# Attention with heads of eight numbers: scores from two f32r parts, stored twice in half of the rows of TensorE's array, in place of three bf16 parts in all of them

## The reference

```python
def causal(x):                       # H=16, Hd=8, L=1024, B=2
    q, k, v = split(layernorm(x) @ W_attn + b_attn)
    scores = einsum('bhqd,bhkd->bhqk', q, k) / sqrt(8)
    scores = where(tril, scores, -inf)
    return einsum('bhqk,bhkd->bhqd', softmax(scores), v) @ W_proj + b_proj

def encoder(x):
    q, k, v = x @ Wq.T + bq, x @ Wk.T + bk, x @ Wv.T + bv     # reshape to 32 heads of [1024, 8]
    att = softmax(einsum('nqd,nkd->nqk', q, k)) + batch_pos
    att_out = einsum('nqk,nkd->nqd', att, v) @ Wo.T + bo
    ...
```

## Time and profile before

| | us |
|---|---|
| runs | 2842.07, 2851.0, 2852.22 (median 2851.0) |
| profiled execution, own time | 2846.07 |
| its span | 2844.2 |
| `a1`: first product of `a1x` to the end of its units | 288.7 to 575 |
| `b1`: SP enters `b1x`, first product, end of its units | 1613.9, 1632.7, 2055 |
| TensorE busy, share of the span | 86% |
| mean granted clock of TensorE | 0.906 |

### The profile page before, as it was taken

The page is one execution under the profiler, slowest core; times in us unless marked ns, Lnnn a source line. Parts: engine busy times, 40 slices in busy tenths (PEclk is TensorE's granted clock), DMA queues, the critical chain, the costliest instruction groups (busy, mean ns, idle before and its releaser), DMA issues. The chain is left out here.

```text
span 2844.2 us, 41392 instructions
## 1 busy us (share of the span) xinstructions
PE 2441.5 (86%) x12171; PEld 1441.7 (51%) x12236; DVE 2095.6 (74%) x4112; ACT 1423.1 (50%) x3001; POOL 623.5 (22%) x605
## 2 busy tenths in 40 slices
PE   5994889949978999779996499899858899969998
PEld 3772344327756555357773322222125555437776
DVE  3994777538968999279995188788337899738998
ACT  2552356615521777146664036666611377616665
POOL 2324000013317000124445100000003400013443
PEclk7996799969979999889997769999978999979999
DMA  1212222112212000034432611211032000004443
GB/s 64 81 55 72 55 61 56 25 36 107 76 37 49 1 1 1 8 128 141 151 144 48 156 43 28 53 29 29 15 39 78 8 1 1 9 7 157 146 151 117
DMA packets 110486, 175.34 MB, mean 62 GB/s; under 512 B 58738, under 2 KB 81138, under 8 KB 98466
## 3 DMA queue, kind: packets, MB, share of 16 engines
q1 hardware_dynamic: 93428, 171.23, 20.7%
q10 hardware_dynamic: 16896, 2.10, 0.5%
HBM read 145.43 MB, written 12.78 MB: 56 GB/s over the span
## 5 line engine op out<-in xcount | busy, mean ns | idle before, releaser
L1496 DVE TENSOR_REDUCE b1x_maxima<-b1x_m_bank 128x1 f32<-128x512 f32 x512 | 317.9, 684 | 82.7 <-PE b1x_m_bank L1414 82.7
L1536 ACT ACTIVATE b1x_probs<-b1x_e_bank 128x1024 f32<-128x1024 f32 x256 | 248.2, 1021 | 119.4 <-PE b1x_e_bank L1432 112.4
L1496 DVE TENSOR_REDUCE a1x_maxima<-a1x_m_bank 128x1 f32<-128x512 f32 (+3 forms) x384 | 190.3, 551 | 72.6 <-PE a1x_m_bank L1417 48.6
L1414 PE MATMUL b1x_m_bank<-b1a_k_slot,b1a_q_slot 96*128 96x512 bf16 x512 | 190.4, 412 | 23.3 <-DMA b1x_v_slot<-b1a_v_aug 20.4
L1536 ACT ACTIVATE a1x_probs<-a1x_e_bank 128x1024 f32<-128x1024 f32 (+1 forms) x192 | 147.3, 809 | 101.4 <-PE a1x_e_bank L1435 79.0
L1432 PE MATMUL b1x_e_bank<-b1a_q_slot,b1a_k_slot 128*128 128x512 bf16 x475 | 145.7, 385 | 8.4 <-issue 4.1
L1414 PE MATMUL a1x_m_bank<-a1a_k_slot,a1a_q_slot 96*128 96x512 bf16 (+3 forms) x384 | 120.2, 351 | 21.2 <-DMA a1x_v_slot<-a1a_v_aug 19.5
L1448 PE MATMUL b1x_o_bank<-b1x_probs,b1x_v_slot 128*32 128x512 f32 x1024 | 137.7, 610 | 0.7 <-ACT b1x_probs L1536 0.7
L1414 PEld LDWEIGHTS b1x_m_bank<-b1a_k_slot,b1a_q_slot 96*128 96x128 bf16 x512 | 41.5, 98 | 181.8 <-DVE b1x_maxima L1496 129.8
L585 ACT ACTIVATE g1e_high<-g1e_hidden 128x512 fp32r<-128x512 f32 x128 | 80.9, 632 | 90.4 <-DVE g1e_hidden L618 90.2
L585 ACT ACTIVATE g2e_high<-g2e_hidden 128x512 fp32r<-128x512 f32 x128 | 81.0, 633 | 90.1 <-DVE g2e_hidden L618 90.0
(11 more groups left out here) (556 smaller groups left out, 6503.7 us busy)
## 6 DMA issues: line engine op xcount, KB each, us to landing
g1e_share<-scratch_combine SPq DMA_DIRECT2D x32, 1024.0 KB, 4.8
g2e_share<-scratch_combine SPq DMA_DIRECT2D x32, 1024.0 KB, 4.8
f1e_share<-scratch_combine SPq DMA_DIRECT2D x9, 1024.0 KB, 4.9
f2e_share<-scratch_combine SPq DMA_DIRECT2D x9, 1024.0 KB, 4.9
b1e_window<-scratch_bias_table SPq DMA_DIRECT2D x16, 320.0 KB, 4.6
a1a_k_slot<-scratch_k_parts SPq DMA_DIRECT2D x24, 192.0 KB
a1a_q_slot<-scratch_q_parts SPq DMA_DIRECT2D x72, 64.0 KB
b1a_k_slot<-scratch_k_parts SPq DMA_DIRECT2D x24, 192.0 KB
```

The costliest lines, as they stand in the source:

```text
L1414: mm = pe.matmul(bank[:, 0:width], q_slot[s][0:MAX_ROW, qt // 4, hh, chunk(qt % 4, 128)], k_slot[s][0:MAX_ROW, hh, k0:k0 + width], start=T ...
L1496: dve.tensor_reduce(maxima[:, k0 // NC, col:col + 1], bank[:, 0:width], AX, ALU.max).then_inc(m_taken, 1)
L1536: act.activation(probs[g % 2][:, 2 * pair:2 * pair + 2, 0:width], e_bank[pair][:, :, 0:width], ACT.Exp, scale=scale).then_inc(exp_done, 1)
```

## The change

- PARTS is 2 and the parts are f32r (ACT makes the high part with the bias added, one DVE operation the low one). Three products of parts by 8 numbers are 24 rows; they are stored **twice** (COPIES = 2), so a head takes 48 rows (MAX_ROW), and the exponential's `scale` is divided by COPIES. The two rows of the maximum follow. Even heads lie in rows 0 to 49, odd ones in rows 64 to 113.
- A score product (lines 1373 and 1391) covers one half of the array's rows; the tiles are ordered by head, so that neighbours lie in different halves. The mask products (1376, 1394) are as before: bf16, over all 128 rows.
- The parts stay on chip. `Narrow.load` copies them from `q_parts` and `k_parts` into the slots: 32 DMAs per group in the causal block, 48 in the encoder (24 for q and 24 for k, of 8x16x64 numbers; a piece that lies together has 64 numbers, 256 bytes). The encoder's weights are permuted on the host so that eight rows of one number index lie together. `v_slot` and its loads go; the value products read `v_aug`.
- Groups 0 and 1 are loaded earlier: group 0 by SP in `qkv_in_parts` (causal) or in the turn of the values (encoder), group 1 by SP in `narrow_values` (causal) or by ACT's queue in `relative_bias` (encoder). Group 2 is loaded at the start of `narrow_attention`, around `rows(0)`.
- No loop: the 16 halves are written out. At every second half SP waits for the end of the half before, loads group + 2, and only then does `rows(half + AHEAD)` (AHEAD is 2 in the causal block and 1 in the encoder) and `store(half)`.
- The first pass is shared out by a planner (`due`: a tile is worth its width + 32, a turn 256): 63 items ahead of the first unit in the causal block, 50 in the encoder, and then about 4.1 per unit in the encoder, none in the last units. Both turns stand six tiles behind the last tile of their half.
- POOL cuts the maximum with two operations in place of five, four DMAs write it.

```diff
-PARTS = 3
+PARTS = 2
+COPIES = 2
+MAX_ROW = 24 * COPIES
...
+    ROW_PARTS = {"q": (0, 1, 0), "k": (0, 0, 1)}
+    def load(self, queue, group, operand):
+        parts, slot = ((self.q_parts, self.q_slot) if operand == "q" else (self.k_parts, self.k_slot))
+        s = group % SLOTS
+        for e in range(4):
+            b, n = (4 * group + e) // NH, (4 * group + e) % NH
+            at = 64 * (e % 2)
+            if self.positions_split:
+                for i in range(3 * COPIES):
+                    part = self.ROW_PARTS[operand][i % 3]
+                    queue.dma_start(slot[s][at + HD * i:at + HD * i + HD, e // 2, :].bitcast(F32),
+                                    parts[:, part, b * L + 64 * n:b * L + 64 * n + 64].bitcast(F32)
+                                    ).then_inc(self.slot_loaded[s], 16)
+                continue
...
-    scale = HD ** -0.5 if causal else 1.0
+    scale = (HD ** -0.5 if causal else 1.0) / COPIES
...
+            narrow.load(sp, 2, "q")
+            rows(0)
+            narrow.load(sp, 2, "k")
+            for half in range(1, AHEAD):
+                rows(half)
+            for half in range(HALVES):
+                group = half // 2 + SLOTS - 1
+                if SLOTS <= group < GROUPS and half % 2 == 0:
+                    sp.wait_ge(pv_done, last_unit[half - 1] + 1)
+                    narrow.load(sp, group, "q")
+                    narrow.load(sp, group, "k")
+                if half + AHEAD < HALVES:
+                    rows(half + AHEAD)
+                store(half)
...
+                rows = slice(64 * (hh % 2), 64 * (hh % 2) + MAX_ROW)
                 diagonal = causal and k0 + width == (qt + 1) * 128
+                mm = pe.matmul(bank[:, 0:width], q_slot[s][rows, hh // 2, chunk(qt, 128)],
+                               k_slot[s][rows, hh // 2, k0:k0 + width], start=True, stop=not diagonal)
                 if diagonal:
                     mm = pe.matmul(bank[:, width - 128:width], ident_bf[:], mask[:, 0, :],
                                    start=False, stop=True)
...
+                for a in ((0, 1) if pair == 0 else (1, 0)):
+                    rows = slice(64 * a, 64 * a + MAX_ROW + PARTS)
                     diagonal = causal and lo == kt * 128
+                    mm = pe.matmul(e_bank[pair][:, a, 0:width], k_slot[s][rows, pair, chunk(kt, 128)],
+                                   q_slot[s][rows, pair, lo:lo + width], start=True, stop=not diagonal)
                     if diagonal:
                         mm = pe.matmul(e_bank[pair][:, a, 0:128], ident_bf[:], mask[:, 1, :],
                                        start=False, stop=True)
```

More of the change, by code:

```diff
@@ L1118, in prepare_values @@
         self.memset(pool, self.v_heads[:, :, :, :, HD], 1.0)
[L1120 to L1128, removed]
 def qkv_in_parts(nc, tag, dram, narrow, h, early, name, v):
     ROT = 6
[L1141 to L1144, removed]
+    items = [(2, n) for n in range(NCH)] if v is not None else []
+    VALUES = len(items)
+    items += [(m, n) for n in range(NCH) for m in range(2)]
     with Phase(nc, tag) as p:
@@ L1385, in _ @@
-            rows(0, 0)
-            def step(it, j, group, last):
-                if not last:
-                    rows(group + 1, (j + 1) % 3)
-            over_groups(pool, step)
-        def count(group, per, index):
-            return group * per + index
+            for half in range(HALVES):
+                into = max_parts[half % 2]
+                pool.wait_ge(m_taken, turn_at[half] + 1)
+                if half >= 2:
+                    pool.wait_ge(rows_set[half % 2], 64 * (half // 2))
+                pool.tensor_copy(into[:, 0, :], rest[:]).then_inc(cut, 1)
+                pool.wait_ge(cut, 2 * half + 1)
+                pool.tensor_tensor(into[:, 1, :], rest[:], into[:, 0, :], ALU.subtract).then_inc(cut, 1)
@@ L1479, in _ @@
-            over_groups(pe, step)
+                scores(0, pair)
+            for u in range(NU):
+                share = list(range(dues[u], dues[u + 1]))
+                for pair in range(2):
+                    if u + 1 < NU:
+                        scores(u + 1, pair)
+                    if pair < len(share):
+                        first_pass(share[pair])
+                values(u)
+                for m in share[2:]:
+                    first_pass(m)
         @block.vector
         def _(dve):
-            dve.sem_inc(m_taken, 3)
@@ L1485, in m_item @@
-            def m_item(group, s, m):
-                item = items[m]
-                dve.wait_ge(m_done, count(group, NM, m + 1))
-                bank = m_bank[(s * NM + m) % 3]
-                if item[0] == "turn":
-                    dve.wait_ge(cut, group * (2 * CUT) + item[1] * CUT + CUT)
+            for m in range(NI):
+                half, qt = items[m][0:2]
+                qh = half % 2
+                dve.wait_ge(m_done, m + 1)
+                bank = m_bank[m % 3]
+                if qt is None:
+                    if half >= 1:
+                        dve.wait_ge(cut, 2 * half)
@@ L1556, in _ @@
-            over_groups(act, step)
+            exponentials(0)
+            for u in range(NU):
+                half = units[u][0]
+                if u + 1 < NU:
+                    exponentials(u + 1)
+                if u == last_unit[half]:
+                    act.wait_ge(pv_done, u + 1)
+                    if half >= 2:
+                        act.wait_ge(o_stored[half % 2], 64 * (half // 2))
+                    act.activation(o_sb[half % 2][:], o_bank[:], ACT.Copy).then_inc(o_copied, 1)
@@ L1833, in _ @@
         def _(act):
-            while narrow.unstored:
-                narrow.store_part(act)
+            narrow.load(act, 1, "q")
+            narrow.load(act, 1, "k")
             for t in range(NT):
```

403 lines of the change are left out of this document (147 added, 256 removed).

## The result

The changed kernel takes 3249.35 us (median of 4 runs, 3241.83 to 3260.66) against 2849.19 of the kernel before (4 runs): a ratio of 1.1411, 95% interval 1.1388 to 1.1433. That is 400 us more, where the forecast was 3094 in a range from 2920 to 3290. The profiled execution took 3241.83 us, the lowest of the four, with a span of 3240.0.

The account below looks back on a forecast made before the run. TensorE was taken to bound both blocks, with DVE close behind in `b1x`. From 2846 us, +205 for `a1x`, +51 for `b1x`, +5 and −13 for the stages before them gave 3094 us, range 2920 to 3290.

Parts of the forecast that it names:

- `b1x`, unit and sum: In `b1x`, 2.85 us per unit with DVE as the bound; 389 us against 421 for the block, −32.
- that apart, as +15: In `b1x`, +15 us for a clock that falls after TensorE has idled in the waits.
- SP's wait: At five group starts in `b1x`, 48 copies issued ahead of the maximum's rows make TensorE wait 13.7 us each: +68.
- The landing: In `b1x`, 1.7 us for landing, within the 36.5 us from a group's start until the maximum's rows are there.
- The round trip: In `a1x`, going from 64-row tiles to full-height masks and back costs 0.30 us, 512 times: +154 us.
- The clock in `a1x`: In `a1x`, draining lowers TensorE's clock: about +250 us at 1.2 GHz throughout, of which +75 was taken.
- the clock stays low in both blocks: Rival: `a1x` +380 us, `b1x` at 3.5 us per unit, +75; the whole about 3345 us. Chance 0.1.
- the forecast's parts: In `a1x` at full clock: pairs −27.5, fewer waits −12, round trips +154, values +9, long turns +3; written as +130.
- The stages ahead: Before the blocks: +5 us in `a1` for SP's copies, −13 in `b1` for a vanished load wait and ACT's issues.
- The other side: Rival: in `a1x` a mask behind its own 64-row product costs no drain; 2858 us (chance 0.06) or 2775 (faster, 0.11).
- the estimate by the Trainium skill: All score products up to twice as fast: −110 us in `b1x`, about −50 in `a1x`, 2686; 0.02 of faster's chance.

Follow-up runs that it names:

- e7: Changed kernel with the maximum's rows issued ahead of a group's loads in `b1x`, and the 48 loads in two lots of 24: 3171.84 us.
- e1: Changed kernel with each diagonal mask product of `a1x` made two 64-row products in the array half of its score product: 2989.11 us.
- e3: Changed kernel with the parts stored once (COPIES = 1), products on 24 rows instead of 48: 3291.31 us.

## Why the prediction was right, and where it was off

The direction, the places and the range were right; the forecast was short by 155 us (148 against the profiled execution, by which the steps are counted here). By its steps:

- **`b1x`, unit and sum: right, by two errors that cancel in part.** 389 us were forecast without the wait; 484.6 − 94.5 = 390 were measured. The unit is 2.70 at full clock (forecast 2.85), and the clock takes the difference back: the units right behind the five waits are some 12 us longer in all than 2.70 each. The forecast had put that apart, as +15.
- **SP's wait: right in place, short in size.** Forecast were five waits of 13.7, 68 us; measured 85.4, and 94.5 with the short ones. The landing was right: the scores go on 34.4 us after SP begins (2111.54 to 2145.96), where 36.5 less the 2 at the start were forecast. What was missed is that TensorE makes the scores a unit ahead of the values, so it wants the rows 17.4 us after SP begins (it stops at 2128.97), not 22.8. e7 takes the wait away.
- **The round trip: right in sum, at full clock by luck.** Forecast 0.30 at full clock and 0.44 at half; measured 0.31 (0.20 out of the 64-row tile and 0.11 into it, on the few products that ran at full clock) and 0.41. At half clock the two parts came as the earlier trace rows had them, 0.29 and 0.11. At full clock the forecast had them the other way round, 0.10 out and 0.19 in. In "TensorEngine Tiling (Array Packing)", section Key Properties, the Trainium skill has a change of tiling mode drain TensorE; the traces agree with that, and add that the drain is 0.19 us longer behind f32r than behind bf16 at half clock.
- **The clock in `a1x`: the step that failed.** "I take a part, +75", between 0 and 250. It was 612 − 415 = 197 us: TensorE stayed at 1.2 GHz for almost the whole block (0.52). The forecast tied the clock to the drains alone. e1 bears that out in part (0.76 without them), and e3 shows that the rows in use bear on it too: 0.50 in `b1x` with TensorE busy for 556 of 560 us. The rival "the clock stays low in both blocks" was right for one of them. Its price there, +380 over before, was 52 above the measured +328. A trip cost 0.03 less than I had, which is 15 of these, and the forecast's parts add up to 126.5 where it wrote 130; the rest I can't place. For `b1x` e3 has the price of a low clock: 4.16 us per unit, where the rival had 3.5.
- **The stages ahead:** +5 and −13 forecast, +11 and −4 measured. In `a1` the mask's own load stood behind the copies, which I had not named. In `b1` I had costed ACT's 48 copies and passed over SP's: in the turn of the values 48 loads of group 0 take 31.6 us on SP where 16 stores took 10.37, and the next stage's own loads stand behind them. That is 21 us later on the queue, about as much as the vanished wait of 20.4 us gives; no run shows that it is what takes it back.
- **The other side** asked for a trip under 0.08 us and is out. Of the estimate by the Trainium skill, "TensorEngine Tiling (Array Packing)", section Theoretical Speedup, the doubled rate is there in the starts of the pairs (0.23 us for two), and in `b1x` DVE takes most of it back, as the forecast had it: 0.35 us per unit are left of 0.86.

Sum: `a1x` +123 over the forecast, `b1x` +13, the stages +15, the tail −3: 148.

## What to carry to other kernels

In this kernel, products on part of the array paid where they stood in runs of their own kind and lost where a full-height product stood behind each of them. That costs 0.3 us at full clock, 154 us for 512 of them, and the lower clock that came with it cost 197 more by the forecast's sum. Before halving a product's rows, ask what the block's bound will be afterwards (in `b1x` it was DVE, 0.35 us per unit away) and whether the granted clock still holds, which only a profile tells. When bulk copies and a small urgent transfer share a queue, cut the bulk into lots that fit in the time in which nothing urgent is ready; whether the urgent one then stood ahead of its lot or behind it made no more than 5 us here.

## What the hardware showed unexpectedly

- Storing the same numbers twice, on 48 rows instead of 24, kept `b1x` at a mean clock of 0.85 instead of 0.50 with the same products on TensorE; 14 further rows of zeros moved it from 0.93 to 0.94 (in `a1x` from 0.78 to 0.84).
- The way from one tile size to another cost 0.30 us at half clock behind an f32r product and 0.11 behind a bf16 one.
- A bf16 mask in the same half, right behind an f32r product on 48 to 64 rows, started 0.10 to 0.12 us after the stream's end at full clock, an f32r mask 0.07 or less. An f32r score product behind another had 0.12 in the first pair behind the values and 0.02 after it; between two masks there was no such gap.
- Products of different halves didn't keep the order of the program. In the program of e1 the two masks of one head stand between its score product and the next one, of the other half, and yet the two products start together (two at 554.87) and the four masks follow (555.19).
- Copies from chip memory to chip memory in pieces of 256 bytes took 0.60 us each to issue on SP (0.65 from start to start), as long as pieces of [32, 8] to DRAM and nearly twice a plain load of 0.33.
